# One exponential for both batches of a block in a selective-scan kernel, with the tanh rows shared out anew

## The reference

```python
A = -exp(soft_clamp(A_log, -5, 5, 0.5))
dt_A = soft_clamp(dt[..., None] * A, -8, 8, 0.5)      # tanh(...) * 16
dA = exp(dt_A)
def step(h, inp):
    h = h * dA_t + dB_t * x_t[:, :, None]
    nrm = sqrt(sum(h * h, axis=(1, 2), keepdims=True))
    fac = minimum(20.0 / (nrm + 1e-08), 1.0)
    h = where(t % 10 == 0, h * fac, h)
    y = einsum('bdn,bn->bd', h, C_t) + D_param * x_t
```

## Time and profile before

| | |
|---|---|
| device time, median of 3 runs | 1750.53 us (1746.51 to 1756.24) |
| the profiled execution | 1753.98 us, span in its trace 1752.2 us |
| mean granted TensorE clock | 0.895 of 2.4 GHz |
| busy over the span | PE 81%, DVE 81%, ACT 75%, POOL 56% |
| 503 to 1483 us, within the scan stage | DVE 925.35 us, ACT 909.13 us, POOL 836.39 us busy of 980 |

### The profile page before, as it was taken

How to read it: one execution, slowest core, us unless ns; L and a number is a source line. 1 busy time by engine, 2 the same in 40 slices (tenths; PEclk the granted TensorE clock), 3 DMA queues, 4 the chain that set the end, 5 groups by cost and what they waited for, 6 DMA issues and landing times.

```text
span 1752.2 us, 23082 instructions
## 1 busy us (share of the span) xinstructions
PE 1410.9 (81%) x6362; PEld 1079.0 (62%) x6362; DVE 1420.5 (81%) x1666; ACT 1319.5 (75%) x3384; POOL 986.2 (56%) x1350
## 2 busy tenths in 40 slices
PE   5999999998277787777777777877777777798987
PEld 4555555553166676666666666766676666677765
DVE  5657666565589999999999999999999998776764
ACT  3466666768999998999999999999999975223332
POOL 0222222211388887888888888888888888200000
PEclk9999999999588888888889889888988888898999
DMA  7222355323144333333433343334423225534430
GB/s 230 72 74 83 113 148 147 106 91 117 47 115 105 80 88 85 101 88 86 104 86 90 90 100 86 89 84 101 105 76 91 81 77 173 160 113 146 142 109 24
DMA packets 202656, 179.78 MB, mean 103 GB/s; under 512 B 82784, under 2 KB 175008, under 8 KB 202528
## 3 DMA queue, kind: packets, MB, share of 16 engines
q1 hardware_dynamic: 199904, 174.11, 35.2%
q10 hardware_dynamic: 2624, 4.19, 0.7%
HBM read 125.26 MB, written 53.57 MB: 102 GB/s over the span
## 4 chain that ended last, share of the span: by engine, by line
PE 31%; ACT 31%; DVE 13%; POOL 11%; issue 10%; DMA 1%; SPq 1%; ACTq 0%; POOLq 0%; DVEq 0%
ACT tb L938 13%; PE banks L895 9%; ACT decay L966 6%; POOL hc L854 6%; DVE h L1055 5%; ACT sc_sq L949 5%; PE banks L1210 4%; PE banks L1221 3%; PE banks L1190 3%; PE banks L339 3%; DVE cv L593 3%; POOL rc L846 3%; PE banks L878 2%; PE banks L354 1%; PE banks L314 1%
## 5 line engine op out<-in xcount | busy, mean ns | idle before, releaser
L1055 DVE TENSOR_TENSOR_SCAN h<-decay,banks 128x704 f32<-128x704 f32 x410 | 661.0, 1612 | 33.9 <-ACT banks L974 28.8
L895 PE MATMUL banks<-hc,w_ident 128*128 128x160 f32 (+1 forms) x3296 | 654.2, 351 | 18.0 <-POOL hc L854 15.0
L854 POOL TENSOR_TENSOR hc<-h,bc 128x640 f32<-128x640 f32 x410 | 592.8, 1446 | 3.5 <-DVE h L1055 3.5
L895 PEld LDWEIGHTS banks<-hc,w_ident 128*128 128x128 f32 x3296 | 563.1, 225 | 42.6 <-POOL hc L854 30.0
L938 ACT ACTIVATE tb<-dtc,a 128x320 f32<-128x320 f32 (+1 forms) x832 | 448.5, 556 | 0.0
L1043 DVE TENSOR_TENSOR banks<-banks,bc 128x640 f32<-128x640 f32 x410 | 341.3, 833 | 34.3 <-DMA bc<-scratch_blk 4.7
L878 PE MATMUL banks<-sc_ss,sc_ones 128*128 128x1 f32 x820 | 167.3, 273 | 248.3 <-ACT sc_sq L949 234.3
L878 PEld LDWEIGHTS banks<-sc_ss,sc_ones 128*128 128x128 f32 x820 | 144.4, 219 | 334.4 <-ACT sc_sq L949 332.1
L966 ACT ACTIVATE decay<-tb 128x640 f32<-128x640 f32 x410 | 298.1, 727 | 0.4
L846 POOL TENSOR_TENSOR rc<-qs,w_mhalf 128x1 f32<-128x1 f32 x410 | 225.7, 550 | 62.0 <-POOL qs L841 1.8
L250 POOL TENSOR_TENSOR ln_rs<-ln_ve,w_mhalf 128x4 f32<-128x4 f32 x8 | 13.9, 1740 | 283.1 <-DVE ln_ve L1409 283.1
(11 more groups left out here) (113 smaller groups left out, 1612.4 us busy)
## 6 DMA issues: line engine op xcount, KB each, us to landing
bc<-scratch_blk SPq DMA_DIRECT2D x205, 320.0 KB, 3.4
uc<-scratch_u SPq DMA_DIRECT2D x35, 240.0 KB, 4.3
scratch_xc<-xc SPq DMA_DIRECT2D x8, 1024.0 KB, 4.8
scratch_sg<-sg SPq DMA_DIRECT2D x8, 1024.0 KB, 5.9
scratch_dt<-dt SPq DMA_DIRECT2D x8, 1024.0 KB, 5.5
scratch_u<-u SPq DMA_DIRECT2D x8, 1024.0 KB, 6.7
q_ys<-scratch_y SPq DMA_DIRECT2D x8, 1024.0 KB, 6.4
q_xc<-scratch_xc SPq DMA_DIRECT2D x8, 1024.0 KB, 9.1
```

The source lines that it names most:

```text
L854: pool.tensor_tensor(hc[:, pl % 2, :, j % 2 * S:(j % 2 + 1) * S] .rearrange("p (c b n) e -> p c b n e", c=KE, b=B)[:, :, b], state(m)[:, : ...
L895: mm = pe.matmul(psY[:, 0:KE * B * wide], w.ident[:], rhs, start=(n == 0), stop=(n == N - 1))
L1055: dve.tensor_tensor_scan(state(m).rearrange("p r e -> p (r e)"), decay[:, m % DRING], psI[m % B][:, 0:NCH * W], 0.0, ALU.mult, ALU.add).th ...
```

## The change

The two Exps of a block (one for each batch, 640 elements) become one of 1280 elements, in the even unit only. It writes two slots of the decay ring and raises `decay_ready` by two. It may start once the scans of both units that used the slots are done. The tanh rows are shared out as one in the even unit and three in the odd one, instead of two and two; at a chunk's last block all four stay in the even unit. Ahead of the loop the four Exps of the first units become two, each before one of the two `copy_q`.

```diff
@@ -749,9 +749,9 @@
         held = tb[:, 0:blocks_of(c), k] if c % 2 == 0 else tb[:, k, 0:blocks_of(c)]
         return held[:, :, :, i, :]
 
-    def tanh_block(j, b):
+    def tanh_pair(j):
         c, k = chunk_of(j)
-        return tb[:, k, :, b] if c % 2 == 0 else tb[:, :, k, b]
+        return (tb[:, k] if c % 2 == 0 else tb[:, :, k]).rearrange("p g b i e -> p b g i e")
 
     def tile_of(t):
         return min(t // TT, TILES - 1)
@@ -956,16 +956,16 @@
                 act.wait_ge(q_held, m - B + 1)
             act.activation(nq[:, b:b + 1], psQ[:, b:b + 1], ACT.Copy).then_inc(q_copied, 1)
 
-        def decays(m):
-            j, b = m // B, m % B
+        def decays(j):
             c, k = chunk_of(j)
-            if k == 0 and b == 0:
+            m = j * B
+            if k == 0:
                 act.wait_ge(tanh_done, (c + 1) * NCH)
             if m >= DRING:
-                act.wait_ge(h_ready, m - DRING + B + 1)
+                act.wait_ge(h_ready, m - DRING + 2 * B)
             act.activation(
-                decay[:, m % DRING].rearrange("p (g i e) -> p g i e", g=DB, e=W)[:, :, :, 1:],
-                tanh_block(j, b), ACT.Exp, scale=DTA_HALF / SHARP).then_inc(decay_ready, 1)
+                decay[:, m % DRING:m % DRING + B].rearrange("p b (g i e) -> p b g i e", g=DB, e=W)[:, :, :, :, 1:],
+                tanh_pair(j), ACT.Exp, scale=DTA_HALF / SHARP).then_inc(decay_ready, B)
 
         def carry(m):
             b = m % B
@@ -988,10 +988,11 @@
 
 
 
+
             c, k = chunk_of((m + AHEAD - B) // B)
             if c + 1 >= DCHUNKS:
                 return c + 1, []
-            half = [k * GR + i for i in range(GR)][m % B * 2:m % B * 2 + 2]
+            half = [k * GR + i for i in range(GR)][m % B:1 + m % B * (GR - 1)]
             if k == blocks_of(c) - 1:
                 half = [k * GR + i for i in range(GR)] if m % B == 0 else []
             if m == 0:
@@ -1003,10 +1004,9 @@
 
         for m in range(B):
             squares(m)
-        for m in range(AHEAD):
-            decays(m)
-            if m < B:
-                copy_q(m)
+        for j in range(AHEAD // B):
+            decays(j)
+            copy_q(j)
         for m in range(B):
             carry(m)
         for m in range(UNITS):
@@ -1023,8 +1023,8 @@
                 copy_q(m + B)
             for r in rows[1:]:
                 tanhs(act, c, r, r + 1)
-            if m + AHEAD < UNITS:
-                decays(m + AHEAD)
+            if m % B == 0 and m + AHEAD < UNITS:
+                decays((m + AHEAD) // B)
             if m + B < UNITS:
                 carry(m + B)
         for p in range((UNITS - 1 - 8) // 4 + 1, PAIRS):
```

## The result

The changed kernel takes 1761.55 us (median of 7, 1756.81 to 1768.13), the one before 1750.53 (median of 7, 1743.13 to 1756.73). The ratio is 1.006, with a 95% interval of 1.0035 to 1.0086: slower by 11 us, 6 to 15. Forecast were 1765 us and a loss of 14. The profiled execution took 1758.50 us with a span of 1756.7, at the low end of its seven; between the scans of units 14 and 404 its scan stage is 8.7 us longer than before (988.7 against 980.0), and what stands behind the last scan is 3.3 shorter.

A forecast was written before the change was run, and what follows sets the result against it. A ring between engines bounds the kernel, DVE's floor of 2.423 us per unit setting the pace. Lost lead 6.6, last blocks 6.5 and half clock 1.2 sum to 14.3 us on the median 1750.53: 1765 us, range 1752 to 1777.

The forecast's parts named there:

- The ring and the floor: Steady laps: DVE's floor stays 2.423 us per unit; the double Exp ends the even lap, `copy_q` to `carry` 1.236 us.
- Rival 3: Steady laps: ACT's ring becomes the bound at over 2.423 us per unit, 1776 us; chance 0.12.
- Rival 2: Steady laps: the double Exp stays hidden under POOL and only the last blocks cost, 1757 us; chance 0.18.
- Rival 4: Scan on DVE: the last blocks are paid from lead, nothing reaches DVE, the time stays at 1751 us; chance 0.10.
- The last blocks: Last block of each of 12 chunks: the double Exp adds 0.54 us to an even unit bound by ACT, 6.5 us.
- The lost lead: Full-clock laps: lead gained per unit falls from 0.035 to 0.013 us; 300 x 0.022 = 6.6 us of disturbances reach DVE.
- Half clock: Even units at the half clock: each gets 0.056 us longer; at most 2.5 us in all, taken as 1.2 us.
- ACT's saving: ACT: the double Exp saves 188 ns per block; busy time falls by some 38 us, which helps nothing.
- The rival "faster": Disturbed units: ACT holds the ring, so its saved 188 ns per block comes through, 1736 us; chance 0.08.
- DVE's idle time: In front of the scan on DVE: idle time 10 to 15 us above the 28.8, with `carry` named.

The follow-up runs named there:

- last_split: The changed kernel, but at the last block of each chunk (12 times) two single Exps, one per unit, instead of the double one: 1755.28 us, ratio 1.0012.
- weigh34_before: The kernel before with POOL's weighing by C left out for one of four channel groups: 1733.58 us, ratio 0.9898.
- no_clamp_before: The kernel before without POOL's clamp of the total (L841), so the factor may be over 1: 1731.60 us, ratio 0.9891.
- rows_early: The changed kernel with tanh rows made one unit earlier, three in the odd unit, the fourth in the next even one, last blocks too: 1737.99 us, ratio 0.9908.
- rows_two_two: The changed kernel with the double Exp, but the tanh rows shared as before, two in each unit: 1872.52 us, ratio 1.0696.
- two_singles: The changed kernel with the double Exp made by two single ones in the same even unit: 1771.45 us, ratio 1.0103.
- singles_spread: The kernel before, single Exps kept, a block's tanh rows reordered: one in the odd unit, two in the next even, one in the next odd: 1767.54 us, ratio 1.0094.

## Why the prediction was right, and what it had wrong

- **The ring and the floor.** DVE's floor didn't move, and the even lap is ended by ACT: `copy_q` to `carry` 1.25 us against 1.236 forecast. The chain with POOL no longer hides it. Rival 3, in which the ring becomes the bound, is out: 9.57 is under 9.69. Rival 2 is wrong in its mechanism, as the Exp isn't hidden, but what it forecast, that only the last blocks cost, is close to what came. Rival 4, in which nothing reaches DVE, is out by the interval of 6 to 15 us.
- **The last blocks**, 12 x 0.54 = 6.5 us. Measured 3.98 - 3.40 = 0.58 a block (0.05 of it a longer wait between the last tanh and the Exp), 7.0 us. DVE stood still 7.5 us longer ahead of these twelve scans, of the 8.7 by which the stage grew, and last_split takes 7.1 of them back. Right, and shown by an experiment.
- **The lost lead**, 6.6 us, is the term that was mis-sized. The failing step: of the odd unit the prediction says "it stays as it was". Its lap fell from 2.38 to 2.34. POOL had set 2.38 by its own round, a path that the prediction didn't have, and the late `carry` of the even unit gives it some hundredths of a us of slack; weigh34_before, which takes POOL's round out of the way, gives the same 2.34 to 2.36. Four laps went from 9.554 to 9.570 us, not to 9.64, so the lead lost per unit is 0.004 us and not 0.022: some 1 us by the prediction's own price. What is left of the stage's 8.7 us without the last blocks is 1.2, and last_split, which has these laps and the old last blocks, is 2 us slower than before with an interval of -2 to +6; both fit. The price itself, the lead lost per unit times 300 units, is not settled: weigh34_before and no_clamp_before gained more than it gives.
- **Half clock**, 1.2 us. The even laps there are 2.61 to 2.63 against 2.56 before, 0.05 to 0.07 as reckoned; its time in the stage went from 257 us of 980.0 to 268 of 988.7, 26% and 27%. Not tested by itself.
- **Sum.** 7.0 + 1 + 1.2 = 9 us against 11 measured and 14.3 forecast. The forecast was right in the sign, in what ends the even lap and in the last blocks. Of its two large terms only one came, and the measured interval of 6 to 15 us holds 9 as well as 14.3: that 1761.55 lies so near to 1765 is in part luck.
- **ACT's saving.** I wrote that ACT's busy time would fall by 38 us; it fell by 17.4. The sum of the Exps did fall by 298.1 - 260.2 = 37.9, but each Exp overlaps the instruction behind it by 0.10 us, and with 205 Exps fewer 20.5 us of such overlap are gone. The prediction used this 0.10 for `carry` and left it out here. Back to back the merging saves 0.09 us a block, not 0.19. The rule in the Trainium skill (ScalarE: Activation LUTs, What ACT_TABLE_LOAD costs) that ACTIVATEs in a row overlap by about 93 ns agrees with the trace: two Exps of 0.727 us take 1.35 together, 0.10 less than their sum.
- **The rival "faster"** fell with the saving: nothing of it reached DVE, whose wait for `carry` rose by 8.0 us.
- **DVE's idle time** was to rise by 10 to 15 us; it rose by 8.0, smaller by the same term.

Not seen in the prediction at all: the merged Exp frees its places a unit earlier. The change as made doesn't use that. rows_early does, and is 24 us faster than the change and 15 faster than before, most of it at the last blocks.

## What to carry to other kernels

In a ring over several engines the mean lap is compared with the floor of the engine that sets the pace; as long as it is below, a lap counts only by the lead that it rebuilds, while a rare lump that is longer than the lead stops the engine each time. Here 12 blocks of 205 made 7 of the stage's 8.7 us, so look for the one block in sixteen that differs before saving in all of them. The steady laps are not free either: 0.07 us less in four laps came with a stage 13 us shorter (weigh34_before), by the lead and in part perhaps by the clock. When one lap of a pair gets longer, work out the other again: an engine that was nearly full may get its slack there. Merging two instructions is worth what they cost back to back less the merged one, not the difference of the shown lengths, and what it frees earlier may be worth more than what it saves.

## What the runs showed of the hardware

- TensorE's granted clock differed between kernels that do the same matmuls. With even laps of 2.86 to 2.93 us (rows_two_two) the mean clock was 0.76 in the stretch in which it was 0.87 before, and PE needed 762 us for 3511 matmuls instead of 754 for 3968; with a shorter ring it was 0.88 to 0.89 (weigh34_before, no_clamp_before). It isn't a plain rule of the lap: two_singles, with four laps of 9.74 us, had 250 us at the half clock in the stage and the kernel before, with 9.55, had 257. So part of a gain or loss may come through the clock, and which part can't be told from these runs.
- Behind the last scan all ten kernels run the same program. It took 241.0 us with 22.5 us at the half clock (rows_early) and 250.0 with 46.2 (singles_spread), and the other eight lie between.
- On ACT, a tanh that waits on a semaphore which the Exp just ahead of it raises starts 0.76 us after it (175 of 187 cases in singles_spread), and `carry`, which doesn't wait for the Exp, 0.64. That the wait for one's own engine costs these 0.12 us is not shown by itself: no run has an Exp with a tanh behind it that doesn't wait.
